# Stage b in one program: the router's instructions merged into the experts' block

## The chip, the cores and the metric

One core of a Trainium2 chip runs the whole kernel. The metric is the device time of one execution in microseconds (us). Engines are named as in the profile: PE (TensorE, matrix products), PEld (its weight loads), DVE (VectorE), ACT (ScalarE), POOL (GpSimd), SP (SyncE, which here only issues DMAs). PSUM is the memory that PE writes to; SBUF is the working memory of the other engines.

## The reference

The input x is 2 sequences of 512 tokens of width 128. Four additions to x follow each other: cross attention to a context of 77 tokens (stage a), a mixture of 8 attention experts (stage b), another cross attention (stage c), and 6 layers of local attention and feed-forward (stage d). The change lies in stage b alone:

```python
h = x @ rW1.T + rb1                       # router, x is layer-normed, width 64
h = relu(layernorm(h) * ln_g + ln_b)
probs = softmax(h @ rW2.T + rb2)          # 8 experts
tp, ti = top_k(probs, 2); tp = tp / tp.sum(-1)
gates = (one_hot(ti, 8) * tp[..., None]).sum(-2)
for e in range(8):                        # every expert is computed for every token
    q, k, v = (x @ w.T + b for ...)       # 16 heads of 8
    o = softmax(q k / sqrt(8)) v          # within each sequence of 512
    out += (o @ ow.T + ob) * gates[e]
```

The router and the experts read the same layer-normed x. The gates are only needed where an expert's output is weighted.

## The kernel before

**Stages.** `build` calls `stage_a`, `stage_b_router`, `stage_b_experts`, `stage_c` and `stage_d`. Each is one block: every engine has its own instruction list in it, and no engine goes on to the next block before all have ended this one. The x of all 8 token tiles (128 tokens each) stays in SBUF as `X`, its normed and transposed copy as `XNT`. PSUM has eight banks: `PA` has four, `PM` two, `PV` and `PX` one each.

**The router** (`stage_b_router`, lines 339 to 461) is a chain in which each step waits for the one before: SP issues ten loads (lines 362 and 364, all signalled on `r_loaded`); `Norm` (lines 112 to 144) normalises X on DVE and transposes it through PE and ACT into XNT; PE multiplies by the router's first weight (L372, `hid`) and makes a constant from all value biases and output weights (L375, `const`); DVE adds the bias, layer-norms the hidden layer and clips it (L418 to L433); PE transposes it and ACT copies it out (L403); PE makes the logits (L383); DVE picks the two best experts and makes the gates (L435 to L457), with one Exp on ACT (L405); PE transposes the gates, ACT copies them (L407), PE makes the base term from gates and constant (L392, `base`), and DVE adds it to X (L461).

**The experts** (`stage_b_experts`) begin, for expert 0, with a preparation: SP loads six weights and biases (L560); PE projects q and k of the first sequence (L683), each drained by ACT (L828) since they share `PX`; POOL splits q and k into three bf16 parts each (`split`, L629 to L636); SP writes the parts to DRAM as 12 DMAs (`take_out`, L575, which waits for `parted`) and, when these have landed and DVE has set KX to one (L936, `keys_set`), reads them back in another layout as 4 DMAs (`bring_in`, L582, "spreading"). Meanwhile PE makes the values (L691) and ACT copies them out (L832) after POOL has cleared VP (L660, L662).

Then 28 score matrices (14 steps of two, `LEAD`) are made one after the other by `query_major` (L722) into the two banks of `PM`, and DVE takes the row maxima of each (`maxima`, L899), which frees the bank. `turn_maxima` transposes the first of them, ACT sends them as rows into QX and KX (L839, L846), and with that the slots begin. A slot is one group of heads: `key_major` (L734) writes scores into all of `PA`, ACT takes the exponentials (L819), PE mixes the values (L744), DVE normalises, and between these stand the score matrices and maxima of a later group. There are 8 slots in an expert (2 sequences by 4 groups) and 8 experts; experts 1 to 6 are a loop. The q and k of the next half expert are projected, split, parked and spread within the slots.

The order on PE before the first slot is written out by hand:

```python
proj(0, 0, "q", 1)
proj(0, 0, "k", 2)
values(0, 0, 3)
pe.wait_ge(keys_set, 1)
for f in range(LEAD):
    query_major(0, f // 8, f % 8)
turn_maxima(0, 0, 4)
for g in range(NG):
    slot(0, g, True, False)
```

Of the kernel before, what the change touches and what calls it, by code (L numbers as in the profile page):

```python
# [13 lines left out]
ALU = mybir.AluOpType  # L14
ACT = mybir.ActivationFunctionType
AX = mybir.AxisListType
# [322 lines left out]
def stage_b_router(nc, shared, d, GATE):  # L339

    with ExitStack() as ctx:
        m = shared.within(ctx)
        X, XNT, PA, PM, PV, PX = m.X, m.XNT, m.PA, m.PM, m.PV, m.PX
        W1, W2, OW = m.sb("RW1", [128, RH]), m.sb("RW2", [RH, NE]), m.sb("ROW", [128, NE * E])
        B1, LG, LB = m.sb("RB1", [128, RH]), m.sb("RLG", [128, RH]), m.sb("RLB", [128, RH])
        B2, RANK = m.sb("RB2", [128, NE]), m.sb("RANK", [128, NE])
        OB, VB = m.sb("ROB", [NE, E]), m.sb("RVB", [128, NE, NE])
        HID, HT = m.sb("HID", [128, NT, RH]), m.sb("HT", [RH, NT * 128])
        LOG, SHIFT, EXP = (m.sb(n, [128, NT, NE]) for n in ("LOG", "SHIFT", "EXP"))
        HIT, PICK = m.sb("HIT", [128, NT, NE]), m.sb("PICK", [128, NT, NE])  # L350
        TOP, REC = m.sb("TOP", [128, NT]), m.sb("RREC", [128, NT])
        GT, C = m.sb("GT", [NE, NT * 128]), m.sb("C", [NE, E])
        norm = Norm(m, "b_norm", X, m.XN)
        names = "loaded hid var std relu turned turned_out logits const shifted exped gated gturned gturned_out cready base added step"
        q = {x: m.sem("r_" + x) for x in names.split()}

        with nc.Block() as block:
            @block.sync
            def _(sp):
                for dst, src in ((W1[:, :], d["rW1T"]), (W2[:, :], d["rW2T"]), (OW[:, :], d["oWT"]), (OB[:, :], d["ob"]),  # L360
                                 (VB[:, :, :], d["vb_diag"]), (RANK[:, :], d["rank"].partition_broadcast(128))):
                    sp.dma_start(dst, src).then_inc(q["loaded"], 16)
                for dst, src in ((B1, "rb1"), (LG, "ln_g"), (LB, "ln_b"), (B2, "rb2")):
                    sp.dma_start(dst[:, :], d[src].partition_broadcast(128)).then_inc(q["loaded"], 16)

            @block.tensor
            def _(pe):
                norm.tensor(pe)
                pe.wait_ge(q["loaded"], 160)
                pe.wait_ge(norm.done, B)  # L370
                for n in range(NT):
                    mm = pe.matmul(PA[:, 0, n * RH:(n + 1) * RH], lhsT=XNT[:, n * 128:(n + 1) * 128], rhs=W1[:, :], start=True, stop=True)  # L372
                mm.then_inc(q["hid"], 1)
                for e in range(NE):
                    mm = pe.matmul(PV[0:NE, 0:E], lhsT=VB[:, e, :], rhs=OW[:, e * E:(e + 1) * E], start=e == 0, stop=e == NE - 1)  # L375
                mm.then_inc(q["const"], 1)
                pe.wait_ge(q["relu"], 1)
                for n in range(NT):
                    mm = turn(m, pe, PM[0:RH, n // TB, (n % TB) * 128:(n % TB + 1) * 128], HID[:, n, :])
                mm.then_inc(q["turned"], 1)  # L380
                pe.wait_ge(q["turned_out"], 1)
                for n in range(NT):
                    mm = pe.matmul(PX[:, n * NE:(n + 1) * NE], lhsT=HT[:, n * 128:(n + 1) * 128], rhs=W2[:, :], start=True, stop=True)  # L383
                mm.then_inc(q["logits"], 1)
                pe.wait_ge(q["gated"], 1)
                for n in range(NT):
                    mm = turn(m, pe, PM[0:NE, n // TB, (n % TB) * 128:(n % TB + 1) * 128], GATE[:, n, :])
                mm.then_inc(q["gturned"], 1)
                pe.wait_ge(q["gturned_out"], 1)
                pe.wait_ge(q["cready"], 1)  # L390
                for n in range(NT):
                    mm = pe.matmul(PA[:, 1 + n // TB, (n % TB) * 128:(n % TB + 1) * 128], lhsT=GT[:, n * 128:(n + 1) * 128], rhs=C[:, :],  # L392
                                   start=True, stop=True)
                mm.then_inc(q["base"], 1)

            @block.scalar
            def _(act):
                s = nc.scalar
                norm.scalar(act)
                act.wait_ge(q["var"], 1)  # L400
                s.activation(m.STD[:, :], m.STD[:, :], ACT.Sqrt).then_inc(q["std"], 1)
                act.wait_ge(q["turned"], 1)
                s.activation(HT[:, :].rearrange("p (b q) -> p b q", b=B), PM[0:RH, :, :], ACT.Copy).then_inc(q["turned_out"], 1)  # L403
                act.wait_ge(q["shifted"], 1)
                s.activation(EXP[:, :, :], SHIFT[:, :, :], ACT.Exp).then_inc(q["exped"], 1)  # L405
                act.wait_ge(q["gturned"], 1)
                s.activation(GT[:, :].rearrange("p (b q) -> p b q", b=B), PM[0:NE, :, :], ACT.Copy).then_inc(q["gturned_out"], 1)  # L407

            @block.vector
            def _(dve):  # L410
                v = nc.vector
                chain = Chain(dve, q["step"])
                link = chain.link
                norm.vector(dve, chain)
                hid, log = [128, NT, RH], [128, NT, NE]
                dve.wait_ge(q["loaded"], 160)
                dve.wait_ge(q["hid"], 1)
                link(v.tensor_tensor(HID[:, :, :], PA[:, 0, :].rearrange("p (n f) -> p n f", n=NT), bc(B1[:, :], 1, hid), ALU.add))  # L418
                for n in range(NT):
                    chain.add(v.bn_stats(m.ST[:, n, :], HID[:, n, :]))  # L420
                chain.wait()
                for n in range(NT):
                    chain.add(v.bn_aggr(m.MV[:, n, :], m.ST[:, n, :]))
                chain.wait()
                v.tensor_scalar(m.STD[:, :], m.MV[:, :, 1], LN_EPS, None, ALU.add).then_inc(q["var"], 1)
                dve.wait_ge(q["std"], 1)
                link(v.reciprocal(m.RSTD[:, :], m.STD[:, :]))
                for n in range(NT):
                    chain.add(v.tensor_scalar(HID[:, n, :], HID[:, n, :], m.MV[:, n, 0:1], m.RSTD[:, n:n + 1], ALU.subtract, ALU.mult))
                chain.wait()  # L430
                link(v.tensor_tensor(HID[:, :, :], HID[:, :, :], bc(LG[:, :], 1, hid), ALU.mult))
                link(v.tensor_tensor(HID[:, :, :], HID[:, :, :], bc(LB[:, :], 1, hid), ALU.add))
# [29 lines left out]

NG = B * HG
LEAD = 14
# [1289 lines left out]
```

## Time and profile before

| What | us |
|---|---|
| Median of 3 runs (2277.52 to 2278.49) | 2277.97 |
| The profiled execution, its own time | 2283.22 |
| Its span in the profile | 2281.3 |
| Stage a | 0 to 120 |
| Router's block | 120.4 to 160.2 |
| Experts, preparation to the first score matrix | 160.5 to 192.3 |
| Experts, first score matrix to the end of the stage | 192.3 to about 1176 |
| Stages c and d | about 1176 to 2281 |

An interval of an expert is taken from one copy of its gates (L932) to the next; there are seven. The profile is of one execution; its time is 5.25 us above the median of the others. In every row of a timeline below the first number is the start in us from the start of the span. "[20.43 <-DMA EKX<-e_park]" is the idle time of the engine ahead of this row and what ended it. "SPq" is the issuing of DMAs, and the end of an issue is not the landing of its data.

### The profile page before, as it was taken

Reading aid. Unit: us, or ns where it says so; the run is one execution under the profiler, and the core shown is the slowest. Engines: PE = TensorE matmul, PEld = TensorE weight load, DVE = VectorE, ACT = ScalarE, POOL = GpSimd, SP = SyncE. Lnnn points to the kernel's source line nnn. Section 1 sums busy time; section 2 is a strip of 40 time slices with the busy share of each in tenths; the row PEclk is TensorE's granted clock in tenths of the full one; section 3 lists DMA queues with packets and bytes.
Section 4 is the critical chain, followed back from the end, with each engine's and each line's share of the span. In section 5 each row is a group of like instructions: output and inputs, shape, how many; then the busy total and the mean of one; then the engine's idle time right before and its main releaser. Section 6 shows DMA issues by size and latency. Waiting matters only on the chain. (4 is left out here: it accounts for less than half of the span.)

```text
span 2281.3 us, 52279 instructions
## 1 busy us (share of the span) xinstructions
PE 1855.1 (81%) x18512; PEld 924.3 (41%) x18512; DVE 1688.7 (74%) x3042; ACT 1277.9 (56%) x1850; POOL 919.9 (40%) x913
## 2 busy tenths in 40 slices
PE   5754888888888888888855888988988988988886
PEld 3530222222222222222223555655655655655654
DVE  4743777767776776777745988977887888877883
ACT  4411665666666665666643656655655655655652
POOL 0002111111111111111015976766776776775770
PEclk9955999989999999999976999999999999999998
DMA  1002323232323232222104333332332332332330
GB/s 35 1 17 56 60 57 62 57 60 56 61 56 60 56 61 56 53 54 48 21 3 121 85 114 85 95 97 77 92 109 77 94 107 77 96 105 68 96 85 10
DMA packets 88745, 152.83 MB, mean 67 GB/s; under 512 B 16819, under 2 KB 51669, under 8 KB 84693
## 3 DMA queue, kind: packets, MB, share of 16 engines
q1 hardware_dynamic: 86421, 149.04, 26.6%
q8 instruction: 136, 2.23, 0.4%
q10 hardware_dynamic: 2112, 0.94, 0.2%
q14 instruction: 76, 0.62, 0.1%
HBM read 98.03 MB, written 51.12 MB: 65 GB/s over the span
## 5 line engine op out<-in xcount | busy, mean ns | idle before, releaser
L899 DVE TENSOR_REDUCE ENM<-PM 128x1 f32<-128x512 f32 x1024 | 657.9, 685 | 252.3 <-PE PM L722 243.8
L819 ACT ACTIVATE EPT<-PA 128x1024 f32<-128x1024 f32 x512 | 512.4, 1021 | 217.4 <-PE PA L734 135.3
L722 PE MATMUL PM<-EKX,EQX 48*128 48x512 bf16 x1024 | 354.6, 400 | 104.4 <-DVE ENM L899 83.7
L1293 POOL TENSOR_TENSOR DRN<-DRN,DHALF 128x8 f32<-128x8 f32 x192 | 354.4, 1846 | 0.0
L1291 POOL TENSOR_TENSOR DQR<-DR 128x512 f32<-128x512 f32 x192 | 253.9, 1323 | 240.6 <-DVE DR L1582 240.6
L642 POOL CAST ENMP<-ENM 128x16 bf16<-128x16 f32 x64 | 12.7, 198 | 782.3 <-DVE ENM L899 782.3
L744 PE MATMUL PV<-EPT,EVP 128*32 128x512 f32 x2048 | 284.4, 628 | 0.8 <-ACT EPT L819 0.8
L722 PEld LDWEIGHTS PM<-EKX,EQX 48*128 48x128 bf16 x1024 | 85.6, 94 | 480.3 <-DVE ENM L899 394.0
L734 PE MATMUL PA<-EQX,EKX 51*128 51x512 bf16 x1024 | 254.1, 396 | 27.2 <-DMA EQX<-EROWS 14.2
L1337 PE MATMUL PM<-DWQKV,DXS 128*128 128x512 f32 x384 | 215.2, 643 | 30.0 <-ACT DRAW L1499 17.5
L1580 DVE TENSOR_TENSOR DR<-DRAW,DTAB 128x512 f32<-128x512 f32 x192 | 184.1, 959 | 32.7 <-DVE Y L1612 11.3
L1499 ACT ACTIVATE DRAW<-PM 128x512 f32<-128x512 f32 x192 | 115.0, 599 | 155.5 <-DVE DR L1582 84.1
L144 PEld LDWEIGHTS PX<-IDENT,DQR 128*128 128x128 f32 x768 | 97.6, 145 | 102.9 <-issue 93.0
L144 PE MATMUL PA<-IDENT,DP 128*128 128x128 f32 x768 | 112.8, 289 | 30.4 <-DVE DP L1608 21.5
L1584 DVE TENSOR_REDUCE DSS<-DSQ 128x8 f32<-128x512 f32 x192 | 129.5, 674 | 0.0
L1407 PE MATMUL PV<-DWO,DOT 128*128 128x128 f32 x768 | 103.0, 291 | 24.1 <-DVE XN L1630 20.9
L1508 ACT ACTIVATE DSQ<-DRAW 128x512 f32<-128x512 f32 x192 | 121.7, 634 | 0.8
L144 PE MATMUL PX<-IDENT,DQR 128*128 128x128 f32 x768 | 118.6, 278 | 3.3 <-ACT DQT L1504 2.7
L144 PEld LDWEIGHTS PA<-IDENT,DP 128*128 128x128 f32 x768 | 90.3, 147 | 68.3 <-DVE DP L1608 41.4
L1297 POOL TENSOR_TENSOR DQR<-DQR,DRN 128x512 f32<-128x512 f32 x96 | 109.7, 1143 | 13.8
L1407 PEld LDWEIGHTS PV<-DWO,DOT 128*128 128x128 f32 x768 | 97.2, 204 | 36.2 <-DVE XN L1630 18.6
L1520 ACT ACTIVATE DPT<-PA 128x512 f32<-128x512 f32 x96 | 52.1, 594 | 92.1 <-PE PA L144 89.4
(209 smaller groups left out, 2894.5 us busy)
## 6 DMA issues: line engine op xcount, KB each, us to landing
DV<-d_vpark SPq DMA_DIRECT2D x192, 256.0 KB, 5.0
d_vpark<-DVT SPq DMA_DIRECT2D x48, 512.0 KB, 2.6
e_park<-EPARTS SPq DMA_DIRECT2D x64, 192.0 KB, 2.9
EQX<-e_park SPq DMA_DIRECT2D x32, 384.0 KB, 5.5
EKX<-e_park SPq DMA_DIRECT2D x32, 384.0 KB, 9.0
DWQKV<-in_WqkvR SPq DMA_DIRECT2D x6, 1536.0 KB, 9.5
e_park<-EPARTS SPq DMA_DIRECT2D x64, 128.0 KB, 2.7
e_park<-EPARTS SPq DMA_DIRECT2D x64, 64.0 KB, 2.1
```

Of the source, the lines that this page charges most:

```text
L144: return pe.matmul(out, lhsT=in_, rhs=m.IDENT[0:k, 0:k], is_transpose=True, start=True, stop=True)
L722: pe.matmul(PM[:, r, :], lhsT=QX[64 * r:64 * r + KQ, b, hp, t * 128:(t + 1) * 128], rhs=KX[64 * r:64 * r + KQ, b, hp, :], start=True, stop ...
L734: mm = pe.matmul(PA[:, 2 * pair + r, :], lhsT=KX[64 * r:64 * r + KS, b, hp, kt * 128:(kt + 1) * 128], rhs=QX[64 * r:64 * r + KS, b, hp, :] ...
L744: mm = pe.matmul(PV[32 * j:32 * j + 32, :], lhsT=VP[:, g // HG, kt, 4 * (g % HG) + j, :], rhs=PT[:, kt, j * S:(j + 1) * S], start=kt == 0, ...
L819: s_.activation(PT[:, kt, pair * 2 * S:(pair + 1) * 2 * S], PA[:, 2 * pair:2 * pair + 2, :].rearrange("p a b -> p (a b)"), ACT.Exp, scale= ...
L899: v.tensor_reduce(NM[:, g % 2, t, j, 0:1], PM[:, r, :], AX.X, ALU.max, negate=True).then_inc(maxed, 1)
L1291: g.tensor_tensor(qr, r1, r2, ALU.add).then_inc(roped.sem if queries else joined.sem, 1)
L1293: g.tensor_tensor(rn, rn, HALF[:, 0:8], ALU.pow).then_inc(rooted.sem, 1)
L1337: pe.matmul(PM[:, 0, :], lhsT=XS[:, b, W + t * 128:W + (t + 1) * 128], rhs=WQKV[:, c * 512:(c + 1) * 512], start=True, stop=True).then_inc ...
L1407: mm = pe.matmul(PV[:, 0:E], lhsT=OT[:, hp, :], rhs=WO[:, hp, :], start=hp == 0, stop=hp == HP - 1)
L1580: v.tensor_tensor(r1, x, bc(tab[:, 0], 1, [128, 8, DL]), ALU.mult).then_inc(step, 1)
L1584: v.tensor_reduce(SS[:, k % 2, :, 0], SQ[:, k % 2, :].rearrange("p (h e) -> p h e", h=8), AX.X, ALU.add).then_inc(summed.sem, 1)
```

## The change

`stage_b_router` and `stage_b_experts` become one function `stage_b` with one block. Each engine's list now holds the router's instructions woven into the experts' preparation:

- SP issues the six expert loads first, then the router's ten, then parks and spreads as before.
- PE does the norm's transposes, q and k, then `hid` and `const`, then the values, then the rest of the router's chain up to `base`, and only then the 28 score matrices. Ahead of the first slot it waits for `added`.
- ACT drains q and k ahead of the router's square root; the values are copied out between the router's HT copy and its Exp.
- DVE sets KX between the norm and the router's bias addition. The addition of the base to X comes after the 28 maxima.
- POOL's list is that of the experts alone; its first `split` no longer waits for the end of the router.
- The router's transposes and logits go to banks 1 to 3 of `PA` in place of `PM` and `PX`.

The diff, cut to its core (the router's own instructions on DVE, unchanged but for the bank of the logits, are left out):

```diff
 [SP]
                 load_qk(0)
                 load(VW, "vWT", 0, v_in)
                 load(OW, "oWT2", 0, o_in)
+                for dst, src in ((RW1[:, :], d["rW1T"]), (RW2[:, :], d["rW2T"]), (ROW[:, :], d["oWT"]), (ROB[:, :], d["ob"]),
+                                 (VB[:, :, :], d["vb_diag"]), (RANK[:, :], d["rank"].partition_broadcast(128))):
+                    sp.dma_start(dst, src).then_inc(q["loaded"], 16)
+                for dst, src in ((RB1, "rb1"), (LG, "ln_g"), (LB, "ln_b"), (RB2, "rb2")):
+                    sp.dma_start(dst[:, :], d[src].partition_broadcast(128)).then_inc(q["loaded"], 16)
                 take_out(0, 0)
                 sp.wait_ge(keys_set, 1)
                 bring_in(0, 0)
 [PE]
+                norm.tensor(pe)
+                pe.wait_ge(norm.done, B)
                 proj(0, 0, "q", 1)
                 proj(0, 0, "k", 2)
+                pe.wait_ge(q["loaded"], 160)
+                for n in range(NT):
+                    mm = pe.matmul(PA[:, 0, n * RH:(n + 1) * RH], lhsT=XNT[:, n * 128:(n + 1) * 128], rhs=RW1[:, :], start=True, stop=True)
+                mm.then_inc(q["hid"], 1)
+                for e in range(NE):
+                    mm = pe.matmul(PV[0:NE, 0:E], lhsT=VB[:, e, :], rhs=ROW[:, e * E:(e + 1) * E], start=e == 0, stop=e == NE - 1)
+                mm.then_inc(q["const"], 1)
                 values(0, 0, 3)
+                pe.wait_ge(q["relu"], 1)
...
+                pe.wait_ge(q["turned_out"], 1)
+                for n in range(NT):
+                    mm = pe.matmul(PA[:, 3, n * NE:(n + 1) * NE], lhsT=HT[:, n * 128:(n + 1) * 128], rhs=RW2[:, :], start=True, stop=True)
+                mm.then_inc(q["logits"], 1)
+                pe.wait_ge(q["gated"], 1)
...
+                pe.wait_ge(q["gturned_out"], 1)
+                pe.wait_ge(q["cready"], 1)
+                for n in range(NT):
+                    mm = pe.matmul(PA[:, 1 + n // TB, (n % TB) * 128:(n % TB + 1) * 128], lhsT=GT[:, n * 128:(n + 1) * 128], rhs=C[:, :],
+                                   start=True, stop=True)
+                mm.then_inc(q["base"], 1)
                 pe.wait_ge(keys_set, 1)
                 for f in range(LEAD):
                     query_major(0, f // 8, f % 8)
                 turn_maxima(0, 0, 4)
+                pe.wait_ge(q["added"], 1)
 [ACT]
+                norm.scalar(act)
                 proj_out(0, 0, "q", 1)
                 proj_out(0, 0, "k", 2)
+                act.wait_ge(q["var"], 1)
+                s_.activation(m.STD[:, :], m.STD[:, :], ACT.Sqrt).then_inc(q["std"], 1)
+                act.wait_ge(q["turned"], 1)
+                s_.activation(HT[:, :].rearrange("p (b q) -> p b q", b=B), PA[0:RH, 1:3, :], ACT.Copy).then_inc(q["turned_out"], 1)
                 act.wait_ge(values_set, 2)
                 values_out(0, 3)
+                act.wait_ge(q["shifted"], 1)
+                s_.activation(EXP[:, :, :], SHIFT[:, :, :], ACT.Exp).then_inc(q["exped"], 1)
+                act.wait_ge(q["gturned"], 1)
+                s_.activation(GT[:, :].rearrange("p (b q) -> p b q", b=B), PA[0:NE, 1:3, :], ACT.Copy).then_inc(q["gturned_out"], 1)
                 rows_out(0, 0, 4)
                 rows_sent(0, 4)
 [DVE]
+                chain = Chain(dve, q["step"])
+                link = chain.link
+                norm.vector(dve, chain)
                 v.memset(KX[:, :, :, :], 1.0).then_inc(keys_set, 1)
+                hid, log = [128, NT, RH], [128, NT, NE]
+                dve.wait_ge(q["loaded"], 160)
+                dve.wait_ge(q["hid"], 1)
...
                 for f in range(LEAD):
                     maxima(0, f // 8, f % 8)
+                dve.wait_ge(q["base"], 1)
+                v.tensor_tensor(X[:, :, :], X[:, :, :], PA[:, 1:3, :].rearrange("p b (t e) -> p (b t) e", t=TB), ALU.add).then_inc(q["added"], 1)
 [build]
-        stage_b_router(nc, shared, d, GATE)
-        stage_b_experts(nc, shared, d, GATE)
+        stage_b(nc, shared, d, GATE)
```

## Rows read from the trace of the kernel before

**Rows 1.** The page of the profile: the span, and the granted clock in 40 slices.

```profile
span 2281.3 us, 52279 instructions
...
PEclk9955999989999999999976999999999999999998
```

**Rows 2.** Timeline, 120 to 160 us, the router (start, us, engine, line, op, idle).

```profile
120.43 0.33 SPq L362 DMA_DIRECT2D RW<-in_rW1T  x1
...
124.70 0.43 SPq L364 DMA_DIRECT2D RB<-in_rb  x1
...
126.84 0.60 ACT L130 ACTIVATE XNT<-PM 128x512 f32<-128x512 f32 x1 [0.43 <-PE PM L144]
...
129.54 3.67 PE L372 MATMUL PA<-RW,XNT 128*128 128x64 f32 x16 [2.73 <-DMA RB<-in_rb]
...
139.18 0.69 DVE L432 TENSOR_TENSOR HID<-HID,RLB 128x512 f32<-128x512 f32 x1
...
143.41 3.58 PE L383 MATMUL PX<-RW,HT 64*128 64x8 f32 x16 [1.11 <-ACT HT L403]
...
155.20 3.78 PE L392 MATMUL PA<-C,GT 8*128 8x128 f32 x16 [1.10 <-ACT GT L407]
159.02 1.22 DVE L461 TENSOR_TENSOR X<-X,PA 128x1024 f32<-128x1024 f32 x1 [6.66 <-PE PA L392]
```

**Rows 3.** Timeline, 160 to 193 us, from the barrier to the first scores.

```profile
160.51 0.33 SPq L560 DMA_DIRECT2D EQW<-in_qWT  x1
...
162.30 6.88 DVE L936 MEMSET EKX<- 128x8192 bf16 x1 [2.06 <-issue]
...
162.84 0.43 SPq L560 DMA_DIRECT2D EOW<-in_oWT  x1
...
164.07 2.08 PE L683 MATMUL PX<-XNT,EQW 128*128 128x512 f32 x2 [5.09 <-DMA EKB<-in_kb]
...
166.93 2.08 PE L683 MATMUL PX<-XNT,EKW 128*128 128x512 f32 x2 [0.78 <-ACT EQ L828]
...
173.55 1.15 POOL L636 TENSOR_TENSOR EPARTS<-EREST,EPARTS 128x512 bf16<-128x512 f32 x1
...
178.56 0.60 ACT L832 ACTIVATE EVP<-PX 128x512 f32<-128x512 f32 x1 [8.83 <-POOL EVP L662]
...
181.17 0.88 SPq L582 DMA_DIRECT2D EKX<-e_park  x2
...
192.29 0.61 PE L722 MATMUL PM<-EKX,EQX 48*128 48x512 bf16 x2 [20.43 <-DMA EKX<-e_park]
```

**Rows 4.** Timeline of DVE alone, 192 us: the 28 first maxima.

```profile
192.91 19.34 DVE L899 TENSOR_REDUCE ENM<-PM 128x1 f32<-128x512 f32 x28 [23.73 <-PE PM L722]
```

**Rows 5.** Timeline of PE alone, 217 to 285 us, an early and a later slot.

```profile
217.66 0.61 PE L734 MATMUL PA<-EQX,EKX 51*128 51x512 bf16 x2 [5.18 <-DMA EQX<-EROWS]
...
228.28 0.60 PE L144 MATMUL PX<-IDENT,ENM 128*12 128x128 f32 x4
...
277.85 0.60 PE L734 MATMUL PA<-EQX,EKX 51*128 51x512 bf16 x2
...
284.89 0.60 PE L144 MATMUL PX<-IDENT,ENM 128*12 128x128 f32 x4
```

**Rows 6.** Busy time by stretch, router and first scores (PEclk is the granted clock).

```profile
132.00:136.00 4.00, 4.00 (x22) 2.84 (x21) 2.58 (x18) 0.00 (x0) 0.00 (x0) 0.59 0.00 0
...
192.00:212.00 20.00, 16.73 (x31) 3.14 (x32) 17.80 (x28) 0.00 (x0) 0.84 (x4) 0.50 0.00 0
...
228.00:232.00 4.00, 3.54 (x28) 0.96 (x24) 3.19 (x6) 1.49 (x2) 2.94 (x4) 1.00 0.68 182
```

**Rows 7.** The same view, the first two of seven expert intervals.

```profile
230.66:345.83 115.17, 99.07 (x620) 26.69 (x614) 87.96 (x156) 75.55 (x87) 19.65 (x48) 1.00 0.27 56
345.83:467.78 121.95, 104.48 (x628) 29.34 (x624) 88.77 (x156) 76.54 (x88) 20.75 (x49) 0.96 0.28 56
```

**Rows 8.** Costliest groups of the page: an addition of stage d, beside POOL.

```profile
L1580 DVE TENSOR_TENSOR DR<-DRAW,DTAB 128x512 f32<-128x512 f32 x192 | 184.1, 959 | 32.7 <-DVE Y L1612 11.3
```

More of the change, by code:

```diff
@@ L516, with stage_b @@
 LAST_USE = use(NE - 1, NG - 1, "avt")
-def stage_b_experts(nc, shared, d, GATE):
+def stage_b(nc, shared, d, GATE):
     with ExitStack() as ctx:
@@ L538, in stage_b_experts @@
         ON, ONT = m.sb("EON", [128, B, TB, E]), m.sb("EONT", [128, S])
+        RW1, RW2, ROW = m.sb("RW1", [128, RH]), m.sb("RW2", [RH, NE]), m.sb("ROW", [128, NE * E])
+        RB1, LG, LB = m.sb("RB1", [128, RH]), m.sb("RLG", [128, RH]), m.sb("RLB", [128, RH])
+        RB2, RANK = m.sb("RB2", [128, NE]), m.sb("RANK", [128, NE])
+        ROB, VB = m.sb("ROB", [NE, E]), m.sb("RVB", [128, NE, NE])
+        HID, HT = m.sb("HID", [128, NT, RH]), m.sb("HT", [RH, NT * 128])
+        LOG, SHIFT, EXP = (m.sb(n, [128, NT, NE]) for n in ("LOG", "SHIFT", "EXP"))
+        HIT, PICK = m.sb("HIT", [128, NT, NE]), m.sb("PICK", [128, NT, NE])
+        TOP, RREC = m.sb("TOP", [128, NT]), m.sb("RREC", [128, NT])
+        GT, C = m.sb("GT", [NE, NT * 128]), m.sb("C", [NE, E])
+        norm = Norm(m, "b_norm", X, m.XN)
+        names = "loaded hid var std relu turned turned_out logits const shifted exped gated gturned gturned_out cready base added step"
+        q = {x: m.sem("r_" + x) for x in names.split()}
         park = nc.dram_tensor("e_park", (B, 2, 2, TERMS, 64, S), BF16, kind="Internal").ap()
@@ new lines, in _ @@
+                for n in range(NT):
+                    chain.add(v.bn_stats(m.ST[:, n, :], HID[:, n, :]))
+                chain.wait()
+                for n in range(NT):
+                    chain.add(v.bn_aggr(m.MV[:, n, :], m.ST[:, n, :]))
+                chain.wait()
+                v.tensor_scalar(m.STD[:, :], m.MV[:, :, 1], LN_EPS, None, ALU.add).then_inc(q["var"], 1)
+                dve.wait_ge(q["std"], 1)
+                link(v.reciprocal(m.RSTD[:, :], m.STD[:, :]))
+                for n in range(NT):
+                    chain.add(v.tensor_scalar(HID[:, n, :], HID[:, n, :], m.MV[:, n, 0:1], m.RSTD[:, n:n + 1], ALU.subtract, ALU.mult))
@@ new lines, in _ @@
+                chain.wait()
+                link(v.tensor_tensor(HID[:, :, :], HID[:, :, :], bc(LG[:, :], 1, hid), ALU.mult))
+                link(v.tensor_tensor(HID[:, :, :], HID[:, :, :], bc(LB[:, :], 1, hid), ALU.add))
+                v.tensor_scalar(HID[:, :, :], HID[:, :, :], 0.0, None, ALU.max).then_inc(q["relu"], 1)
+                dve.wait_ge(q["logits"], 1)
+                link(v.tensor_tensor(LOG[:, :, :], PA[:, 3, 0:NT * NE].rearrange("p (n e) -> p n e", n=NT), bc(RB2[:, :], 1, log), ALU.add))
@@ new lines, in _ @@
+                dve.wait_ge(q["exped"], 1)
+                link(v.tensor_tensor(EXP[:, :, :], EXP[:, :, :], PICK[:, :, :], ALU.mult))
+                link(v.tensor_reduce(TOP[:, :], EXP[:, :, :], AX.X, ALU.add))
+                link(v.reciprocal(RREC[:, :], TOP[:, :]))
+                v.tensor_tensor(GATE[:, :, :], EXP[:, :, :], bc(RREC[:, :], 2, log), ALU.mult).then_inc(q["gated"], 1)
+                dve.wait_ge(q["const"], 1)
+                v.tensor_tensor(C[:, :], ROB[:, :], PV[0:NE, 0:E], ALU.add).then_inc(q["cready"], 1)
```

138 lines of the change are left out of this document (22 added, 116 removed).

## The prediction

> **What bounds the kernel now.** I read the page first. Its span is 2281.3 us, and its row of granted clocks shows one long low patch, in the third and fourth of 40 slices, about 114 to 228 us [rows 1]. The chain of waits comes next and says nothing here: its listing reaches back only into stage d, past the changed part. So the changed stretch is read from the timeline, where the question at each row is what it waited for.
>
> The router is one chain without overlap. XNT is complete at 126.84 + 0.60 = 127.44; PE then waits for the router's ten loads until 129.54 and starts `hid`; the last of its steps, `base`, ends at 155.20 + 3.78 = 158.98, and the addition to X ends at 160.24 [rows 2]. After the barrier the experts begin at 160.51 with six loads. q is projected at 164.07, k ends at 166.93 + 2.08 = 169.01, POOL has split both at 174.70, the last spreading DMA is issued at 181.17, and the first score matrix starts at 192.29 after 20.43 us in which PE waits for that data [rows 3]. From there on the work is one stream of score matrices and slots. So two serial chains bound this stretch: the router's, 120.43 to 160.24, and the preparation's, 160.51 to 192.29. They share only XNT.
>
> **Which chain is longer once they run side by side.** First the preparation. In the new order q needs XNT (127.44) and its weights; these took 164.07 - 160.51 = 3.56 us from the first issue [rows 3], so they land at 120.43 + 3.56 = 123.99 and XNT decides. q starts at 127.5. From q to the first score matrix took 192.29 - 164.07 = 28.22 us, so the spread data is there at 127.5 + 28.2 = 155.7. SP's share of this is free: the last of the router's ten issues starts at 127.5 (below), before POOL has split q, so the parking DMAs queue behind nothing. KX must be set too: DVE's memset takes 6.88 us and came 2.06 us late to its place [rows 3]; even behind the start of the second XNT copy and with that delay it ends at 126.84 + 2.06 + 6.88 = 135.8, before `hid` can end.
>
> Then the router. Two things push it back. SP issues six loads ahead of its ten, 162.84 + 0.43 - 160.51 = 2.76 us [rows 3]; the last router load was issued at 124.70 and the wait for all ended 4.84 us later [rows 2], which now gives 127.46 and 132.30. And PE projects q and k first: 127.5 + (169.01 - 164.07) = 132.44. Both run together, so `hid` starts at 132.44, 2.90 us later than the 129.54 of before. All that follows moves with it and `base` ends at 158.98 + 2.90 = 161.88. What is woven in beside it:
> - The values, on PE between `const` and the transposes of the hidden layer. DVE's work covers them: `hid` now ends at 136.1, DVE needs until about 139.87 + 2.9 only to add the last bias [rows 2], and PE would be idle. Cost 0; without that cover, some 2 us, about one projection [rows 3].
> - The copy of the values on ACT, 0.60 us [rows 3], sits ahead of the router's Exp. The logits' matmuls, 3.58 us [rows 2], hide it. Its wait for POOL's cleared VP ends at 127.5 + (178.56 - 164.07) = 142.0, before the transposed hidden layer is due (143.41 + 2.9, less the copy). Cost 0.
> - Draining q and k on ACT ends by 133.2, well before the router's square root is due. Cost 0.
> - The addition to X, 1.22 us [rows 2], leaves the chain. It goes behind the 28 maxima, which take 19.34 us back to back [rows 4], and ends at about 162.5 + 19.3 + 1.2 = 183.1. PE waits for it ahead of the first slot, whose first `key_major` waited for rows sent by DMA until 217.66 [rows 5], in the new time 187.3. Cost 0 with 4.2 us in hand.
>
> So the router is the later chain by 161.9 - 155.7 = 6.2 us, the spread data waits for PE, and the first score matrix starts at 161.9 in place of 192.29. **That is 30.4 us less.**
>
> **Three costs that no row shows directly.**
> - DVE beside POOL. The router's DVE work used to run alone; now POOL splits k and clears VP until 142.0, over 142.0 - 136.1 = 5.9 us of it. An addition of 512 elements from two SBUF inputs took 0.69 us in the router [rows 2] and 0.959 us on average in stage d, where POOL is busy [rows 8], 1.39 times as much. Bounds: 0, and 5.9 x (1 - 1/1.39) = 1.7 us if all DVE work suffers so. I take 0.3, one such addition (0.27), because statistics and small operations read one tensor. By the Trainium skill (GPSIMD Engine Reference, Key points) POOL shares its SBUF interfaces with VectorE, with contention where a VectorE instruction has two SBUF inputs or reads one through two ports; by it the scaling of the eight hidden tiles would suffer too, and the sum would be nearer its upper bound. The other way round, POOL could be slowed; 6.2 us are there for it.
> - PE's clock. In 132 to 136 us PE was busy throughout and the granted clock averaged 0.59, between its two levels of 1.2 and 2.4 GHz [rows 6], so it rose late in that stretch. The new order keeps PE busy over the same time. Bounds: 0, and half of `hid`'s 3.67 us, a gain of 1.8. I take a gain of 0.3, since the rise came in the last microsecond.
> - The entry of the block. DVE's first instruction of the experts came 2.06 us after it could [rows 3]. If this delay moves ahead of the norm it lies on the chain; before it was off the chain, since KX was not what PE waited for. Bounds 0 to 2.1 lost; I take 0, because the norm's block did not show it.
>
> The sum is 30.4 - 0.3 + 0.3 = 30.4 us. The profiled execution took 2283.22 us, and would take 2252.8; the median of the runs lies 5.25 below it, and the same saving gives 2277.97 - 30.4 = **2247.6 us**. Everything from the first score matrix on is taken as unchanged and only earlier.
>
> **Rivals.**
> 1. The clock comes back earlier. Before, PE was idle for 20 us ahead of the first score matrices, and these then ran at clock 0.50 throughout with PE busy 16.73 of 20 us [rows 6]; DVE set their pace, so nothing was lost there. But the first slot was slow: from its first `key_major` to its transposed maxima 228.28 - 217.66 = 10.62 us, against 284.89 - 277.85 = 7.04 us in a later slot with the same projections at clock 1.00 [rows 5, 6]. The new order puts `base`, 3.78 us of solid work, right ahead of the scores. If this raises the clock and it holds, 3.6 us more go: 2244.0 us. Against it: 84% busy did not raise it. The Trainium skill (TensorE: Matmul & The Clock Gate, Part 1) says that sustained activity releases the throttle and idling restores it, which speaks for this rival. Chance 0.15.
> 2. The low stretches in the experts fall otherwise. The interval of the first expert took 115.17 us at clock 1.00, that of the second 121.95 at 0.96 [rows 7]. PE loses its clock after a wait for DMA in some experts and not in others; a shift of the whole stage may add or save one such stretch, up to 6.8 us: 2241 or 2254 us. For the unchanged pattern speaks that three runs agree within 1 us. Chance 0.15.
> 3. The preparation becomes the later chain, or DVE suffers in full. The spreading would have to land over 6.2 us later than reckoned. DVE at its upper bound and the entry delay give 30.4 - 1.7 - 2.1 = 26.6 us saved, 2251.4 us. Chance 0.08.
> 4. Slower than before. One mechanism: the shift makes PE drop to the lower clock at waits in the experts that it now passes at full clock. At 0.96 mean clock, 8% of 121.95 us, 9.8 us, was spent at the lower level, and cost up to 6.8 us [rows 7]. To lose 30.4 + 4.6 us needs some 50 us more at the lower level, five more such stretches over eight experts. Nothing in the waits themselves changes. Chance 0.02.
>
> **How the numbers follow.** My forecast with its small terms (2245.5 to 2250.5) has a chance of 0.60. Rivals 1 and 2 stretch the range down to 2241 and up to 2254, and the bounds of the unknown terms lie within it; I give 2240 to 2254. A measurement of this kernel tells about 0.2%, 4.6 us, from no change. Only rival 4 and what I have not foreseen end on the slower side: faster 0.96, same 0.01, slower 0.03.
>
> **What would show it.** Right: q at about 127.5 us, `hid` at 132.4, the spread data landed at 155.7, `base` ending near 161.9 and the first score matrix within 0.5 us of it, not released by DMA; X added near 183; the first `key_major` at 187.3, still waiting for its rows. Rival 1 shows as clock 1.00 before 187 us; rival 2 as expert intervals other than before; rival 3 as a first score matrix that waits for EKX or a chain from `hid` to `base` longer than 29.4 us. The prediction is wrong if the first score matrix starts after 165 us or if stages c and d change their length.

## The result, and the profile after

The changed kernel took 2257.26 us (median of 4 runs, 2250.62 to 2258.53) against 2277.74 us of the kernel before (4 runs, 2274.3 to 2278.49): a ratio of 0.9901, 95% interval 0.9877 to 0.9926. Faster, by 16.9 to 28.0 us, where 30.4 had been forecast; the time lies above the forecast range of 2240 to 2254. Two later comparisons of the same two kernels gave 0.9883 (0.9833 to 0.9932) and 0.9894 (0.9859 to 0.9929). In the first of these one run of the changed kernel, 2275.82 us, lay over 1.5% above the kernel's fastest and is left out of the ratio.

The page of the kernel after, where the low patch of the clock is shorter than in [rows 1], the fourth slice at 0.7 in place of 0.5:

```profile
span 2254.4 us, 52269 instructions
...
PEclk9957999989999999999968999989999999999998
```

The timeline of the changed block, all engines (start us, us, engine, line, op, idle before):

```profile
118.62 1.64 DVE L112 BATCH_NORM_STATS2 ST<-X 128x6 f32<-128x128 f32 x8 [0.31 <-PEq L180]
...
125.66 2.08 PE L565 MATMUL PX<-XNT,EQW 128*128 128x512 f32 x2 [0.69 <-ACT XNT L130]
...
130.38 3.51 PE L678 MATMUL PA<-RW,XNT 128*128 128x64 f32 x16
...
136.21 3.51 POOL L542 MEMSET EVP<- 128x4096 f32 x1
136.54 3.21 DVE L869 TENSOR_SCALAR STD<-MV 128x8 f32<-128x8 f32 x1
...
142.74 0.88 SPq L459 DMA_DIRECT2D EKX<-e_park  x2
...
158.91 3.77 PE L699 MATMUL PA<-C,GT 8*128 8x128 f32 x16 [1.10 <-ACT GT L796]
162.62 0.61 PE L604 MATMUL PM<-EKX,EQX 48*128 48x512 bf16 x2
163.26 19.35 DVE L818 TENSOR_REDUCE ENM<-PM 128x1 f32<-128x512 f32 x28 [7.19 <-PE PM L604]
...
182.53 1.21 DVE L907 TENSOR_TENSOR X<-X,PA 128x1024 f32<-128x1024 f32 x1
...
188.10 0.61 PE L616 MATMUL PA<-EQX,EKX 51*128 51x512 bf16 x2 [5.27 <-DMA EQX<-EROWS]
```

The reader is to see three things. The first score matrix at 162.62 follows `base` at once and waits for no DMA; 20.43 us of waiting are gone [rows 3]. The addition to X ends at 183.74 and the first `key_major` still waits for its rows. And in the middle stands what no step had foreseen: a TENSOR_SCALAR (each element of one tensor combined with a scalar) on 8 elements per partition takes 3.21 us. In the router of before the same instruction took 0.17. From the timeline of the kernel before, the start of the block and this instruction:

```profile
120.46 1.64 DVE L112 BATCH_NORM_STATS2 ST<-X 128x6 f32<-128x128 f32 x8 [0.31 <-PEq L180]
...
135.87 0.17 DVE L425 TENSOR_SCALAR STD<-MV 128x8 f32<-128x8 f32 x1
...
136.55 1.87 DVE L429 TENSOR_SCALAR HID<-HID,MV,RSTD 128x64 f32<-128x64 f32 x8
```

Where the time went, from the starts of the blocks in the two profiles. In this execution the changed block starts 1.84 us earlier, though nothing ahead of it was changed. From the block's start, its first DVE instruction (120.46 before, 118.62 after), to the first maximum on DVE (192.91, 163.26) it is 72.45 against 44.64 us: **27.8 us less**. The experts, from the first maximum to stage c, took 5.9 us more (983.2 and 989.1), stage c the same 35.8, stage d 3.1 us less (1069.3 and 1066.2). The sum is the 26.9 us between the spans. So the changed part gained less than forecast by 2.6 us, and parts that the change does not touch moved by more than that.

### The profile page after: what moved, and what is told of

Read it like the earlier page. It is cut to its first block and busy times, and to the rows that moved or that the text cites. A ratio compares the mean times of both kernels' runs of the same rounds, so it can differ in the third digit from the quotient of the medians.

```text
span 2254.4 us, 52269 instructions
## 1 busy us (share of the span) xinstructions
PE 1849.5 (82%) x18512; PEld 917.4 (41%) x18512; DVE 1690.9 (75%) x3042; ACT 1276.8 (57%) x1850; POOL 920.1 (41%) x913
## 3 DMA queue, kind: packets, MB, share of 16 engines
q1 hardware_dynamic: 86421, 149.04, 27.1%
## 5 line engine op out<-in xcount | busy, mean ns | idle before, releaser
L616 PE MATMUL PA<-EQX,EKX 51*128 51x512 bf16 x1024 | 256.4, 398 | 27.1 <-DMA EQX<-EROWS 14.8
```

The source lines that it names most:

```text
L616: mm = pe.matmul(PA[:, 2 * pair + r, :], lhsT=KX[64 * r:64 * r + KS, b, hp, kt * 128:(kt + 1) * 128], rhs=QX[64 * r:64 * r + KS, b, hp, :] ...
```

## The experiments

### The changed kernel, again and again

No edit. It was run to learn by how much one execution differs from the next.

> The changed kernel as it is, for what one execution differs from the next. Theory A (the experts lose clock by where the stage falls on the chip's own time grid, the same in each execution): the first score matrix again about 44.0 us after the block's first instruction, the experts (first score matrix to the start of stage c) again about 989.7 us, the expert intervals within 1 us of the first profile's 119.3, 120.5, 122.3, 119.7, 119.6, 122.9, 123.6. Theory B (the intervals are drawn anew each time): the intervals differ by several us from those. Ratio to the kernel before 0.990.

2252.97 us median of 6 (2232.17 to 2275.82), ratio 0.9883. The first maximum came 44.64 us after the block's start, to the hundredth as before. The intervals from expert to expert were 119.2, 123.7, 119.6, 122.5, 119.8, 120.5 and 118.8, up to 4.8 us off the first profile's. Theory B holds: they are drawn anew. Stage d took 1056.6 us, 9.6 less than in the first profile.

> The changed kernel a third time, to tell how far its executions lie apart. If the executions differ by how long PE runs at its lower clock, the first 44.6 us of the stage (block start to first maximum) are the same again within 0.3 us, and the experts take 927 us plus 0.285 us for each us at the lower clock, as over the six profiles so far, within 3 us. If the change itself lengthened the experts, they take over 985 us again, whatever the clock.

2252.0 us median of 6 (2244.21 to 2263.7). First maximum after 44.65 us, as expected. The experts took 983.9 us, so they did not stay above the 985 named as the sign that the change lengthens them. The kernel before was profiled again beside it:

> The kernel before, a second profile. First maximum again 72.4 us after the start of the router's block, within 0.3; experts 927 us plus 0.285 us per us at the lower clock, within 3 us; an expert interval differs by several us from the first profile's if the low stretches are drawn anew in each execution.

First maximum after 72.94 us (72.45 the first time), which is outside the 0.3 us allowed: PE's wait for the router's loads ended 9.51 us after the block's start in place of 9.08. Experts 986.4 us. Busy time by stretch shows what the executions differ in. Each pair of rows is first the experts from 40 us after their first maximum to stage c, then stage d; the third number from the right is the granted clock. The kernel before, first and second profile:

```profile
232.91:1176.13 943.22, 808.72 (x4897) 227.70 (x4896) 682.48 (x1200) 602.62 (x693) 150.25 (x361) 0.97 0.26 52
1211.96:2281.30 1069.34, 896.46 (x12816) 606.10 (x12816) 869.35 (x1597) 601.03 (x1034) 736.80 (x519) 0.95 0.33 90
```

```profile
233.47:1179.86 946.39, 811.55 (x4901) 228.42 (x4897) 683.52 (x1201) 603.13 (x693) 150.44 (x361) 0.96 0.26 52
1215.69:2274.90 1059.21, 885.61 (x12816) 598.84 (x12816) 869.76 (x1597) 600.22 (x1034) 736.65 (x519) 0.96 0.33 91
```

The changed kernel, first and third profile:

```profile
203.26:1152.34 949.08, 815.06 (x4896) 227.88 (x4896) 681.99 (x1198) 601.71 (x692) 149.82 (x361) 0.96 0.26 52
1188.17:2254.40 1066.23, 887.42 (x12816) 600.55 (x12816) 869.07 (x1597) 600.46 (x1034) 737.47 (x519) 0.96 0.33 90
```

```profile
205.96:1149.87 943.91, 809.19 (x4896) 227.86 (x4893) 681.69 (x1198) 601.75 (x692) 150.47 (x361) 0.97 0.26 52
1185.70:2242.30 1056.60, 884.59 (x12816) 599.86 (x12816) 867.93 (x1597) 600.09 (x1034) 739.60 (x519) 0.96 0.33 91
```

DVE, ACT and POOL do the same work in the same time throughout; PE's busy time and its clock go with the length. That the clock is the cause of the length is my reading of this; e6 below tests it in part. Between the two levels, a mean clock of 0.96 over 949 us means about 76 us at the lower one. A line through all 13 profiles of this study, of nine different kernels, gives 926 us plus 0.29 us for each us at the lower level, correlation 0.93. The rounded clock makes the time at the lower level coarse, steps of 19 us, so the slope is an estimate. By whole experts (first maximum to stage c) the kernel before took 983.2 and 986.4 us, the changed one 989.1, 985.4 and 983.9: no lengthening by the change can be told. From the block's start to stage c it is 1057.5 us on the mean of two against 1030.8 on the mean of three, 26.7 us less.

### Is it POOL that holds the small instruction?

Edit of e1, and what goes with it on ACT:

```diff
 [POOL]
                 split(0, 0, 1)
+                pool.wait_ge(q["relu"], 1)
                 gp.memset(VP[:, :, :, :, :], 0.0).then_inc(values_set, 1)
 [ACT]
-                act.wait_ge(values_set, 2)
-                values_out(0, 3)
                 act.wait_ge(q["shifted"], 1)
                 s_.activation(EXP[:, :, :], SHIFT[:, :, :], ACT.Exp).then_inc(q["exped"], 1)
+                act.wait_ge(values_set, 2)
+                values_out(0, 3)
```

> POOL's clearing of VP waits for relu, so that it no longer runs beside the router's normalisation on DVE. Theory (POOL's memset holds DVE's small two-port TENSOR_SCALAR): the TENSOR_SCALAR on STD takes 0.17 us in place of 3.21, and hid start to base end shrinks by 3.0 us, from 32.3 to 29.3. Rival (that instruction is slow for a reason of its own, as the merged block's code or PE's matmuls): it stays at 3.2 us wherever POOL is. The whole time falls by 3 us or, if the experts' low clock depends on where they start, by anything between 0 and 9.

Timeline of e1, DVE, POOL and PE:

```profile
140.53 0.17 DVE L870 TENSOR_SCALAR STD<-MV 128x8 f32<-128x8 f32 x1
...
145.07 3.51 POOL L543 MEMSET EVP<- 128x4096 f32 x1 [4.79 <-DVE HID L878]
...
163.59 0.61 PE L605 MATMUL PM<-EKX,EQX 48*128 48x512 bf16 x2
```

The instruction is back at 0.17 us and the first maximum comes after 41.63 us instead of 44.64: 3.01 us, as expected. The time was 2249.51 us median of 6 (2246.71 to 2252.81), ratio 0.9879 (0.9853 to 0.9906); against the changed kernel's 0.9883 the gain of 3 us cannot be seen in the time, only in the trace.

e3 puts a second, equal memset of VP behind the first (ACT waits for one signal more):

```diff
                 gp.memset(VP[:, :, :, :, :], 0.0).then_inc(values_set, 1)
                 pool.wait_ge(values_set, 1)
+                gp.memset(VP[:, :, :, :, :], 0.0).then_inc(values_set, 1)
+                pool.wait_ge(values_set, 2)
```

> The changed kernel with VP cleared twice, 3.5 us more of POOL memset beside the router's normalisation; the result is the same. Theory (memset on POOL holds two-port work on DVE): the router's chain from hid to base grows by 3.5 us, to 35.8, seen as one TENSOR_SCALAR held at STD and another in the scaling of the hidden tiles. Rival (the 3.2 us belong to that one instruction): the chain stays at 32.3.

```profile
140.00 3.51 POOL L542 MEMSET EVP<- 128x4096 f32 x1
140.32 3.22 DVE L871 TENSOR_SCALAR STD<-MV 128x8 f32<-128x8 f32 x1
...
143.57 3.51 POOL L544 MEMSET EVP<- 128x4096 f32 x1
143.81 0.20 DVE L873 RECIPROCAL RSTD<-STD 128x8 f32<-128x8 f32 x1 [0.28 <-ACT STD L790]
144.05 4.25 DVE L875 TENSOR_SCALAR HID<-HID,MV,RSTD 128x64 f32<-128x64 f32 x8
```

First maximum after 47.05 us, 2.41 more than 44.64. The row to look at is the last: the scalings of the eight hidden tiles took 4.25 us in place of 1.87. The reciprocal ahead of them, beside the same memset, is not held. I had expected 3.5 us; 0.5 us of the memset had passed when the scalings began, and of the remaining 3.0 they lost 2.4.

e7 puts the clear, in the order of e1, beside the picking of the experts, to see which instructions are held:

```diff
+                pool.wait_ge(q["shifted"], 1)
                 gp.memset(VP[:, :, :, :, :], 0.0).then_inc(values_set, 1)
```

> As e1, but POOL's clearing of VP waits for shifted, so that it runs beside the small two-input TENSOR_TENSORs that pick the experts (0.22 to 0.23 us each). Theory C (POOL's memset holds every DVE instruction that reads two SBUF inputs or uses two ports): the first of them takes 3.2 to 3.5 us, the chain is 3.0 to 3.5 us longer than in e1, first maximum 44.6 to 45.1 us after the block's start. Theory D (it holds only single-input TENSOR_SCALARs): the two-input ones keep 0.23 us and only L896 or L895, the TENSOR_SCALAR on HIT, is held for the rest of the clear, about 2 us, first maximum near 43.5. Rival: nothing is held, 41.6.

```profile
149.96 3.51 POOL L543 MEMSET EVP<- 128x4096 f32 x1 [12.00 <-DVE SHIFT L882]
150.01 0.22 DVE L890 TENSOR_TENSOR HIT<-LOG,TOP 128x64 f32<-128x64 f32 x1
150.26 0.22 DVE L891 TENSOR_TENSOR HIT<-HIT,RANK 128x64 f32<-128x64 f32 x1
150.52 0.22 DVE L892 TENSOR_REDUCE TOP<-HIT 128x8 f32<-128x64 f32 x1
...
151.04 0.23 DVE L894 TENSOR_TENSOR PICK<-PICK,HIT 128x64 f32<-128x64 f32 x1
151.30 2.22 DVE L896 TENSOR_SCALAR HIT<-HIT 128x64 f32<-128x64 f32 x1
153.53 0.32 POOL L545 MEMSET EVP<- 128x128 f32 x1
```

Theory D, to the tenth: four TENSOR_TENSORs (two tensors combined, here both in SBUF) and a reduction pass beside the memset at their usual 0.22 to 0.23 us, the first TENSOR_SCALAR is held until it ends at 153.47, and the first maximum comes after 43.41 us. The Trainium skill (Advanced Engine Details and Errata, VectorE Performance Modes, Mode Summary) says that VectorE's second SBUF port is shared with GpSimd, and that two-port instructions and those of GpSimd block each other. The rows agree for TENSOR_SCALAR with both operands in SBUF. That its input goes through two ports is the page's reading; the trace shows only who is held and until when.

e7 settles this for a memset, which reads no tensor. It does not show that a TENSOR_TENSOR passes beside every instruction of POOL, and the trace of the kernel before shows that it does not. Its stages c and d, which no edit here touches, have holds of both kinds:

```profile
1176.09 10.46 POOL L966 MEMSET DV<- 64x6144 f32 x2 [23.92 <-POOLq L556]
...
1178.48 2.86 DVE L117 TENSOR_SCALAR STD<-MV 128x8 f32<-128x8 f32 x1
...
1181.85 6.39 DVE L121 TENSOR_SCALAR XN<-X,MV,RSTD 128x128 f32<-128x128 f32 x8
...
1241.93 1.27 POOL L1291 TENSOR_TENSOR DQR<-DR 128x512 f32<-128x512 f32 x1
1242.08 1.67 DVE L1580 TENSOR_TENSOR DR<-DRAW,DTAB 128x512 f32<-128x512 f32 x1 [1.32 <-POOL DQR L1297]
...
1245.14 0.69 DVE L1580 TENSOR_TENSOR DR<-DRAW,DTAB 128x512 f32<-128x512 f32 x1
1245.23 1.73 POOL L1291 TENSOR_TENSOR DQR<-DR 128x512 f32<-128x512 f32 x1
```

At the start of stage c the same TENSOR_SCALAR on 8 elements took 2.86 us beside a memset, and the eight scalings behind it 6.39 us, where the norm ahead of the router needs 0.17 and 2.14 us for the same two (at 122.81 and 123.50). In stage d the addition of two SBUF tensors that began 0.15 us behind a TENSOR_TENSOR of POOL took 1.67 us; the one that began 0.09 us ahead of it took 0.69, and there it was POOL's that took longer, 1.73 us against the 1.27 of the one before.

### Can the router start sooner?

e2 is e1 with three moves: the loads of V and O go behind the router's, `hid` goes between q and k on PE, and the values go behind the logits.

```diff
 [SP]
-                load(VW, "vWT", 0, v_in)
-                load(OW, "oWT2", 0, o_in)
...
+                load(VW, "vWT", 0, v_in)
+                load(OW, "oWT2", 0, o_in)
                 take_out(0, 0)
 [PE]
                 proj(0, 0, "q", 1)
-                proj(0, 0, "k", 2)
...
                 mm.then_inc(q["hid"], 1)
+                proj(0, 0, "k", 2)
...
-                values(0, 0, 3)
...
                 mm.then_inc(q["logits"], 1)
+                values(0, 0, 3)
```

> As e1, and the router's loads go ahead of those of V and O, PE does hid between q and k, and the values come after the logits. Theory (the router's chain is the later one, with slack on the preparation): hid starts 1.5 to 1.8 us sooner, first score matrix 39.3 us after the block's start against 44.0 in the changed kernel, and still not released by DMA, since k is some 3 us later and the preparation had 8 us in hand. Rival (the preparation is now as long): the first score matrix waits for EKX and starts no sooner than in e1 (41.0).

Four rows of its timeline:

```profile
135.97 3.99 DVE L874 TENSOR_SCALAR HID<-HID,MV,RSTD 128x64 f32<-128x64 f32 x8
136.03 1.15 POOL L513 TENSOR_TENSOR EREST<-EQ,EPARTS 128x512 f32<-128x512 f32 x1
137.35 0.61 POOL L516 CAST EPARTS<-EREST 128x512 bf16<-128x512 f32 x1 [0.17 <-POOL EREST L513]
138.04 1.20 POOL L518 TENSOR_TENSOR EPARTS<-EREST,EPARTS 128x512 bf16<-128x512 f32 x1
```

`hid` ended 1.33 us sooner after the block's start than in e1, but the first maximum came after 42.38 us, later than e1's 41.63. Neither theory: the preparation was not the bound, the router's own chain had grown. The split of k, pushed back by 2.8 us, now ran beside the eight scalings, and these took 3.99 us in place of 1.87. Three of the eight are long, one beside each of POOL's instructions above: 1.26, 0.63 and 1.14 us, where none took over 0.32 in e1. So POOL's cast and subtractions hold TENSOR_SCALAR too, each at most for its own length. The spread data had landed at 156.84, 3.6 us before the first score matrix at 160.44. The time was 2250.74 us median of 6 (2243.15 to 2264.17), ratio 0.9887 (0.9852 to 0.9922).

### One program without the overlap

e4 leaves the block merged but puts q, k and the values behind `base`, and their drains on ACT likewise (only the lines added on PE are shown):

```diff
 [PE]
                 pe.wait_ge(norm.done, B)
-                proj(0, 0, "q", 1)
-                proj(0, 0, "k", 2)
...
                 mm.then_inc(q["base"], 1)
+                proj(0, 0, "q", 1)
+                proj(0, 0, "k", 2)
+                values(0, 0, 3)
```

> The merged block with q, k and the values of expert 0 put behind base on PE and ACT: one program, but nothing of the preparation beside the router's chain except loads and the memset of KX. Theory (the gain is the overlap): first maximum about 69.5 us after the block's start, against 72.45 in the kernel before and 44.64 in the changed one; 3 us of the 27.8 belong to the loads that come early and to the barrier. Rival (the barrier and code entry are a good part of the gain): below 65 us.

```profile
162.42 2.08 PE L565 MATMUL PX<-XNT,EQW 128*128 128x512 f32 x2
...
190.31 0.61 PE L604 MATMUL PM<-EKX,EQX 48*128 48x512 bf16 x2 [20.10 <-DMA EKX<-e_park]
```

First maximum after 68.73 us, and the wait for the spread data is back; 69.5 us had been expected. The merge alone (loads early, no barrier, X added later) gives 72.45 - 68.73 = 3.7 us; the overlap gives the other 24.1, and would give 27.1 without POOL's hold. One execution took 2275.5 us.

### The addition to X ahead of the maxima

e5 is the changed kernel with the last addition of the router moved back in front of the 28 maxima.

```diff
+                dve.wait_ge(q["base"], 1)
+                v.tensor_tensor(X[:, :, :], X[:, :, :], PA[:, 1:3, :].rearrange("p b (t e) -> p (b t) e", t=TB), ALU.add).then_inc(q["added"], 1)
                 for f in range(LEAD):
                     maxima(0, f // 8, f % 8)
-                dve.wait_ge(q["base"], 1)
-                v.tensor_tensor(X[:, :, :], X[:, :, :], PA[:, 1:3, :].rearrange("p b (t e) -> p (b t) e", t=TB), ALU.add).then_inc(q["added"], 1)
```

> The changed kernel with the addition of base to X ahead of the 28 maxima on DVE, where the changed kernel has it behind them. As reckoned in the prediction it costs nothing behind them; ahead of them its 1.22 us lie on the chain: first maximum 45.9 us after the block's start against 44.64, less if PE's first score matrix is made meanwhile (0.6 us of it): 45.2 to 45.9. Rival (the chain is held by something else): 44.6.

First maximum after 45.25 us, 0.61 more, the lower end: PE makes the first score matrices during half of the addition. Behind the maxima it costs nothing on the chain. (e3, e5 and e7 were timed once each, at 2255.2, 2251.42 and 2248.44 us, too little to compare by time.)

### Where PE loses its clock in the experts

In nearly every expert PE waits 0.8 to 2.9 us at the start of the third slot for the rows that ACT's queue sends (L616 here, the same wait as in the first slot). These DMAs are under way together with the spreading and the weights of the next half; that this makes them late was not tested. In the changed kernel's first profile:

```profile
220.85 0.61 PE L616 MATMUL PA<-EQX,EKX 51*128 51x512 bf16 x2 [1.60 <-DMA EQX<-EROWS]
```

```profile
216.00:220.00 4.00, 2.86 (x19) 0.59 (x17) 2.58 (x4) 3.10 (x4) 0.00 (x0) 1.00 0.68 101
220.00:224.00 4.00, 2.79 (x11) 0.58 (x15) 1.97 (x3) 1.94 (x2) 0.00 (x0) 0.56 0.00 0
224.00:228.00 4.00, 3.65 (x20) 0.56 (x16) 2.19 (x5) 2.09 (x3) 0.83 (x4) 0.50 0.00 0
```

The clock falls to its lower level at this wait. Of the nine low stretches that begin between 200 and 1140 us of this profile seven begin at this wait or within 2.1 us behind its end. The other two follow another wait, for ACT's copy EONT:

```profile
867.27 1.15 PE L592 MATMUL PX<-EOW,EONT 128*128 128x128 f32 x8 [1.32 <-ACT EONT L764]
```

Behind it the granted clock averaged 0.62 over the stretch from 868 to 872 us.

e6 is e1 with work for PE ahead of the wait for the rows. The wait for `exped` moves ahead of it, since the spare products write to PA:

```diff
+                    if not (isinstance(f, int) and f < 2):
+                        pe.wait_ge(exped, f - 1)
+                    if s == 0 and g == 2:
+                        for _ in range(6):
+                            pe.matmul(PA[:, 0, :], lhsT=KX[0:KQ, b, hp, 0:128], rhs=QX[0:KQ, b, hp, :], start=True, stop=True)
                     if s == 0:
                         pe.wait_ge(rows_in, (e * NG + g) * 64 + 64)
-                    if not (isinstance(f, int) and f < 2):
-                        pe.wait_ge(exped, f - 1)
```

> As e1, and ahead of the wait for the rows at the start of each third slot PE makes six score matrices that nobody reads (the next ones write over them), 1.2 to 1.3 us at full clock. Theory (the lower clock in the experts begins at this wait, 1.0 to 2.9 us of idle PE in each expert): the low stretches behind the third slot's start vanish, the experts shrink from about 984 to 970 us, the time by some 14 us, and the runs lie closer together. Rival (the low stretches come from elsewhere, or six matrices cost PE what they save): the experts stay at 982 to 995 us, or grow by 8 x 1.3 = 10 us.

> e6 a second time, since one profile of it cannot settle what six spare matrices do to the low stretches. Theory: low time in the experts again below the 57 to 96 us of the other profiles (37.5 the first time), experts 975 to 980 us, ratio to the kernel before 0.984 to 0.988. Rival (the first was luck): low time 57 us or more, experts 983 us or more.

The experts of the two profiles of e6, from 40 us after the first maximum:

```profile
201.58:1139.26 937.68, 809.33 (x4944) 230.88 (x4941) 681.40 (x1198) 601.30 (x692) 149.85 (x361) 0.98 0.26 53
```

```profile
204.38:1138.01 933.63, 804.99 (x4941) 229.18 (x4933) 680.84 (x1198) 601.26 (x692) 150.46 (x361) 0.98 0.26 53
```

Clock 0.98 in both, against 0.95 to 0.97 in the eleven other profiles. From the first maximum the experts took 977.7 and 973.6 us; in the others 982.1 to 994.9. The times were 2246.04 us (6 runs, 2234.79 to 2258.76; ratio 0.9854, 0.9815 to 0.9893) and 2246.45 us (6 runs, 2242.41 to 2252.47; ratio 0.9869, 0.9837 to 0.9900). The first expectation holds in its direction alone: the experts shrank, but not to 970 us, the ratio fell by 0.0025 against e1's, some 6 us and not 14, and the six runs lie 24 us apart, e1's 6. Of the second, written after the first profile of e6, the low time and the ratio hold; the experts took 1.4 us less than the 975 to 980 named. Waits over 0.8 us at this place were left in the first expert alone (1.06 and 1.98 us). Low stretches became fewer but did not vanish, so these waits are a cause of them and not the only one. e6 has the lowest medians of all kernels here, 30 to 36 us below the kernel before in its two comparisons, but the intervals overlap with those of e1 and of the changed kernel. In both profiles of e6 stage d was long (1072.2 and 1069.4 us), with the clock at 0.95; in the other kernels it took 1056.6 to 1069.3. Whether that is chance is open. It takes back all of what the experts gained in one profile and half in the other: from the first maximum to the end they took 2085.7 and 2078.8 us, the profile of e1 2083.7.

## Why the prediction was wrong, point by point

- **Which chain is longer: right.** q started 7.04 us after the block's first DVE instruction, as reckoned (127.5 - 120.46). The last spreading DMAs were issued 17.1 us after q, as before (181.17 - 164.07) [rows 3], and landed by 153.5, 34.9 us into the block, against 35.2 reckoned; the first score matrix did not wait for them. e2 was meant to find the limit of this slack and did not.
- **`hid` 2.9 us later: right, a little pessimistic.** It ended at 133.89, 15.27 us into the block, against 15.65 reckoned.
- **The values, their copy and the drains at no cost: right.** From the end of `hid` to the end of `base` nothing on the chain but the one held instruction is longer: 28.8 us against 25.8 before [rows 2], and e1 takes these 3.0 us back. (A chain from the start of `hid` to the end of `base` above 29.4 us was named as the sign of rival 3; it was 32.3. Its mechanism was there, at another instruction and price.)
- **The addition to X: right.** It ended 65.1 us into the block, 62.6 reckoned plus the 2.6 by which all of it came later; e5 shows the 0.6 us that it would cost elsewhere.
- **"DVE beside POOL": the first failed step.** The term was taken at 0.3 us, with a bound of 1.7, by scaling the work of 5.9 us with the slowdown of an addition in stage d [rows 8]. It measured 3.04 us. Two readings were wrong. It is no slowdown in proportion but a wait for the end of POOL's instruction, so its bound is the length of that instruction, 3.51 us for the memset, however small the held one is. The mean of 0.959 us in stage d hid this: it mixes additions of 0.67 to 0.69 us with held ones of up to 1.68. And what the memset holds is not the addition with two SBUF inputs, which e7 shows to pass, but TENSOR_SCALAR. The small operations that I excluded were the ones hit. That a small TENSOR_SCALAR waits for a memset's end could have been read from the trace of before, at the start of stage c, where the same instruction took 2.86 us.
- **The clock in `hid`, a gain of 0.3: a small gain, for another reason.** `hid` took 3.51 us in place of 3.67, but the granted clock was 0.50 from its start to its end in both kernels (129.54 to 133.21 before, 130.38 to 133.89 after). The rise in [rows 6] came after `hid` had ended and could not have shortened it. What differs is that `hid`'s first weights were loaded at 129.61, while PE still made k. That the sum came near here is luck.
- **The block's entry, 0: right.** The delay of 1.65 us ahead of the memset of KX was off the chain.
- **The sum.** 41.4 us from the block's start to the first score matrix had been reckoned, 44.0 were measured: + 3.0 for the hold, - 0.4 for `hid`. The saving in the changed part was 27.8 instead of 30.4 us. That shortfall alone, 2.6 us, would have put the time at 2250.2 us, inside the range.
- **The range: the second failed step, and the larger.** "Three runs agree within 1 us" was taken as a sign that the pattern of the clock stays, and one odd interval more or less as all that could move. The profiled execution, 5.25 us above that median, already spoke against it. Over all comparisons the kernel before ran from 2266.4 to 2290.2 us and the changed one from 2232.2 to 2263.7. Even without the 3.0 us of the hold the median of 2257.26 would have lain at 2254.2, just above the range. Against a median that wanders by several us, a forecast of the mechanism right to 3 us needed a range of some 10 us to each side. Rival 2 was at work, but not as a shift that the change brings: both kernels have it in every execution. The sign "stages c and d change their length" was no sign for the same reason: stage c took 35.8 us in both, but stage d 1069.3 and 1059.2 us in two profiles of the kernel before. The measured 20.5 us between the first medians is 7 below the 27.8 of the traces; the third comparison's ratio of 0.9894 is 24 us, and 27.8 us would be 0.9878, inside all three intervals. That the rest is the clock is inferred from the profiles; the timed runs have no trace of their own.
- **Rival 1 did not come.** The first score matrices ran at 0.50 as before, and the clock stayed there until 196 us, past the 187 named as the sign. `base` right ahead of them did not raise the clock.

## What to carry to other kernels

When work of another engine is moved beside DVE's chain, look which of DVE's instructions are TENSOR_SCALARs in SBUF and how long POOL's instructions beside them are: each can wait for the whole of one (2.22 us of 3.51 in e7, 3.21 in the changed kernel). Beside POOL's TENSOR_TENSORs look at DVE's additions of two SBUF tensors too. A wait on a semaphore that DVE's chain sets anyway can move a memset out of the way, as in e1, where it cost nothing that the trace shows. Look for holds that are there already: in stage c of both kernels the two TENSOR_SCALAR steps behind the memset take 6.9 us more than in the router's norm (2.86 - 0.17 and 6.39 - 2.14), and PE waits for them. That is an estimate of what moving this memset could give; no run tests it. Measure such a change in the trace of the changed stretch, from a fixed event to a fixed event, which repeated here to 0.01 us in three profiles of the changed kernel (to 0.5 in two of the kernel before) while the whole time wandered by over 10. And take the spread of a kernel from many runs and from its profile, not from three runs that happen to agree.

## What was not expected of the hardware

- A DVE TENSOR_SCALAR of 8 elements per partition, 0.17 us, took 3.20 to 3.22 us in five profiles in which POOL's memset of 3.51 us had begun 0.3 us before it, and 0.17 in the profiles where it had not. Reciprocals, reductions and TENSOR_TENSORs passed beside the same memset (e3, e7). DVE's own memset of KX in bf16 took 6.88 us in both kernels [rows 3], with POOL's casts beside it; a cast beside it took 0.61 us (128.62 in the changed kernel) and one behind its end 0.61 too (132.42).
- Stage a, which no kernel here touches, ended at 118.6 to 122.8 us: 4 us of difference before the changed code is reached. In the changed kernel's first profile PE's clock came back ahead of its last products there and in the kernel before it did not; beyond these two the cause was not looked at.
